# First loads and first products of a fused two-layer transformer kernel: keys' inputs loaded in four pieces each, products interleaved, bias row later, half the warm-up matmuls

## The reference, cut to what matters

```python
x = x + tanh(g_xattn[0]) * L0_xattn(layernorm(x), ctx, ctx)        # causal attention, 16 heads of 32
x = x + tanh(g_ffn[0])   * L0_ffn(layernorm(x), w_gate_up, w_proj) # weights rounded to -1, 0, 1 by groups of 64
x = x + tanh(g_xattn[1]) * L1_xattn(layernorm(x), ctx, ...)        # projections q, k_img, v_img, o
x = x + tanh(g_ffn[1])   * L1_ffn(layernorm(x), w_norm, w_gv, w_out)
```

## Time and profile before

| | us |
|---|---|
| median of 3 runs | 1070.06 (1070.04 to 1070.12) |
| profiled execution, whole time | 1070.2 |
| its span, first to last instruction | 1068.4 |
| PE busy | 1037.9 (97%) |
| DVE busy | 832.5 (78%) |
| ACT busy | 585.7 (55%) |
| POOL busy | 119.4 (11%) |

### The profile page before, as it was taken

How to read it: one execution, slowest core, us unless ns; L and a number is a source line. 1 busy time by engine, 2 the same in 40 slices (tenths; PEclk the granted TensorE clock), 3 DMA queues, 4 the chain that set the end, 5 groups by cost and what they waited for, 6 DMA issues and landing times.

```text
span 1068.4 us, 24253 instructions
## 1 busy us (share of the span) xinstructions
PE 1037.9 (97%) x9685; PEld 616.8 (58%) x9770; DVE 832.5 (78%) x1440; ACT 585.7 (55%) x893; POOL 119.4 (11%) x212
## 2 busy tenths in 40 slices
PE   8899999999999999999999999999999999999998
PEld 3555555555777777777777664444444444444444
DVE  4988888878777675675666487798898989888987
ACT  4766777677443332333333357647585858583633
POOL 1101001010000000000000211221111111110110
DMA  9575554542331130321311032224343434331223
GB/s 363 172 256 173 195 182 138 187 146 74 121 80 45 46 80 1 80 65 36 80 32 49 20 93 57 62 47 91 80 90 80 90 79 89 78 69 44 41 59 80
DMA packets 121200, 102.77 MB, mean 96 GB/s; under 512 B 94721, under 2 KB 95233, under 8 KB 120833
## 3 DMA queue, kind: packets, MB, share of 16 engines
q1 hardware_dynamic: 121088, 101.21, 34.4%
HBM read 65.54 MB, written 12.58 MB: 73 GB/s over the span
## 4 chain that ended last, share of the span: by engine, by line
PE 82%; DVE 9%; issue 4%; ACT 2%; DMA 2%; SPq 0%; POOL 0%; ACTq 0%; DVEq 0%; POOLq 0%
PE bank L704 10%; PE bank L705 10%; PE bank L792 10%; PE bank L669 9%; PE bank L810 9%; PE bank L918 7%; PE bank L936 4%; PE bank L906 4%; PE bank L869 3%; PE bank L891 2%; PE bank L549 2%; PE bank L606 2%; PE bank L574 2%; PE bank L622 2%; PE bank L634 2%
## 5 line engine op out<-in xcount | busy, mean ns | idle before, releaser
L704 PE MATMUL bank<-ARENA,W 128*128 128x256 f16 x1024 | 227.3, 273 | 0.7 <-issue 0.7
L705 PE MATMUL bank<-ARENA,W 128*128 128x256 f16 x1024 | 227.3, 273 | 0.0
L1111 ACT ACTIVATE ARENA<-ARENA 128x512 f16<-128x512 f32 (+1 forms) x96 | 66.8, 707 | 140.1 <-DVE ARENA L1759 132.0
L918 PE MATMUL bank<-W,ARENA 128*128 128x512 bf16 x496 | 115.8, 379 | 3.1 <-DMA ARENA<-ARENA 0.6
L810 PE MATMUL bank<-ARENA 128*128 128x512 f32 x256 | 118.4, 603 | 0.2 <-DVE ARENA L1846 0.2
L669 PE MATMUL bank<-ARENA 128*128 128x512 f32 x256 | 117.8, 602 | 0.7 <-DMA ARENA<-in_wkv 0.7
L792 PE MATMUL bank<-W,ARENA 128*128 128x512 bf16 x478 | 114.1, 379 | 2.6 <-DVE ARENA L1765 0.6
L704 PEld LDWEIGHTS bank<-ARENA,W 128*128 128x128 bf16 x1024 | 100.2, 98 | 19.2 <-issue 1.1
L705 PEld LDWEIGHTS bank<-ARENA,W 128*128 128x128 bf16 x1024 | 100.2, 98 | 17.9
L2224 POOL TENSOR_TENSOR ARENA<-ARENA 128x2 f32<-128x2 f32 (+1 forms) x72 | 51.7, 718 | 481.0 <-DVE ARENA L1533 249.1
L1759 DVE SCALAR_TENSOR_TENSOR ARENA<-bank,ARENA 128x512 f32<-128x512 f32 x64 | 48.0, 749 | 65.7 <-PE bank L705 62.3
(11 more groups left out here) (190 smaller groups left out, 1730.8 us busy)
## 6 DMA issues: line engine op xcount, KB each, us to landing
W<-in_w SPq DMA_DIRECT2D x48, 512.0 KB, 4.2
ARENA<-in_w SPq DMA_DIRECT2D x24, 512.0 KB, 3.6
kv_store<-ARENA SPq DMA_DIRECT2D x32, 256.0 KB, 4.4
W<-kv_store SPq DMA_DIRECT2D x15, 512.0 KB, 4.5
ARENA<-in_ctxT SPq DMA_DIRECT2D x8, 512.0 KB, 3.8
X<-in_x SPq DMA_DIRECT2D x8, 512.0 KB, 6.7
ARENA<-in_ctx SPq DMA_DIRECT2D x8, 512.0 KB, 6.2
out<-X SPq DMA_DIRECT2D x15, 256.0 KB, 2.3
```

Of the source, the lines that this page charges most:

```text
L704: pe.matmul(bank[:, i * S:(i + 1) * S], W0[:, at:at + P], xt_half(b, 0)[:, k, :], start=(k == 0), stop=False)
L705: mm = pe.matmul(bank[:, i * S:(i + 1) * S], W0[:, at:at + P], xt_half(b, 1)[:, k, :], start=False, stop=(k == KD - 1))
L918: mm = pe.matmul(to, QQ[d][:, t, k * P:(k + 1) * P], W1[:, at:at + D], start=(k == 0), stop=(k == KD - 1))
L1111: return act.activation(to, src, ACT.Copy)
```

## The change

`load_keys(0)` and the two halves of the key weights become eight smaller loads: for each `k` of 0 to 3, the 256 columns of the turned context and the 512 columns of the weights that step `k` needs. The bias row goes from between them to behind the columns. The products of the two token tiles are interleaved: step 0 of both, step 1 of both, and so on, and each step waits for its own two pieces. The warm-up has five matmuls in place of ten. There are three new semaphores; nothing else is computed or moved.

```diff
-            load_keys(0)
-            sp.dma_start(bufA["wkv"][:, 0, 0:2 * D], wkv[:, 0:2 * D]).then_inc(s.ld_wk, 16)
-            sp.dma_start(keep["row"], vec[:, 0:D]).then_inc(s.ld_kb, 16)
-            sp.dma_start(bufA["wkv"][:, 0, 2 * D:KD * D], wkv[:, 2 * D:KD * D]).then_inc(s.ld_wk2, 16)
+            for k, (keys, weights) in enumerate(((s.ld_p0, s.ld_p0), (s.ld_p1, s.ld_wk), (s.ld_p2, s.ld_p2), (s.ld_kt0, s.ld_wk2))):
+                sp.dma_start(bufA["KT"][:, k, :], ctxT[:, k * S:(k + 1) * S]).then_inc(keys, 16)
+                sp.dma_start(bufA["wkv"][:, 0, k * D:(k + 1) * D], wkv[:, k * D:(k + 1) * D]).then_inc(weights, 16)
             load_x(0)
             sp.dma_start(pre["cst"], cst).then_inc(s.ld_cst, 16)
             sp.dma_start(keep["gate"], gates).then_inc(s.ld_gc, 16)
             sp.dma_start(keep["cols"], cols).then_inc(s.ld_gc, 16)
+            sp.dma_start(keep["row"], vec[:, 0:D]).then_inc(s.ld_kb, 16)
             load_w0(0)
...
-                pe.wait_ge((s.ld_wk, s.ld_wv)[what], 16)
-                pe.wait_ge((s.ld_kt0, s.ld_kt1)[b % 2], 16 * (b // 2 + 1))
+                if (b, what) != (0, 0):
+                    pe.wait_ge((s.ld_wk, s.ld_wv)[what], 16)
+                    pe.wait_ge((s.ld_kt0, s.ld_kt1)[b % 2], 16 * (b // 2 + 1))
...
                 for k in ks:
-                    if not what and k == 2:
-                        pe.wait_ge(s.ld_wk2, 16)
+                    if (b, what) == (0, 0):
+                        for landed, pieces in (((s.ld_p0, 2),), ((s.ld_p1, 1), (s.ld_wk, 1)), ((s.ld_p2, 2),), ((s.ld_kt0, 1), (s.ld_wk2, 1)))[k]:
+                            pe.wait_ge(landed, 16 * pieces)
...
-            for n in range(10):
+            for n in range(5):
                 pe.matmul(banks[7], bufA["MHL"][:, 0, :], bufA["MHL"].rearrange("p a b -> p (a b)"), start=True, stop=True)
-            a_project(0, 0, 0)
-            a_project(0, 0, 1)
+            for k in range(KD):
+                a_project(0, 0, 0, (k,))
+                a_project(0, 0, 1, (k,))
```

More of the change, by code:

```diff
@@ L39 @@
 Sems = namedtuple("Sems", """
-    ld_cst ld_gc ld_x0 ld_x1 ld_kt0 ld_kt1 ld_rv0 ld_rv1 ld_w00 ld_w01 ld_w02 ld_w1a ld_w1b ld_wk ld_wk2 ld_wv ld_sel ld_wqo ld_kb ld_row ld_wn
+    ld_cst ld_gc ld_x0 ld_x1 ld_kt0 ld_kt1 ld_rv0 ld_rv1 ld_w00 ld_w01 ld_w02 ld_w1a ld_w1b ld_wk ld_wk2 ld_p0 ld_p1 ld_p2 ld_wv ld_sel ld_wqo ld_kb ld_row ld_wn
 ld_k0 ld_k1 ld_v0 ld_v1 st_kv0 st_kv1 st_out0 st_out1
```

## The result

The changed kernel takes 1072.33 us (median of 14 runs, 1071.47 to 1075.47) against 1070.09 of the kernel before (14 runs, 1069.59 to 1073.06). The ratio is 1.0023, interval 1.0016 to 1.0031. The forecast was 1070.4 and its range ended at 1071.5, so it was wrong. The runs fall into groups: six lie at 1071.5 to 1071.6, five between 1072.0 and 1073.9, and three at 1075.3 to 1075.5. The profiled execution is one of the last group (1075.47, span 1073.7). The mean clock granted to TensorE sorts them too: the four runs in which it is 1.000 all lie at 1071.47 to 1071.62, the ten with 0.997 or 0.998 reach from 1071.61 to 1075.47.

The account below looks back on a forecast made before the run. PE's own work, busy 97% of the span, was taken as the bound, with only the start movable. Scores gained 0.1, but the later store's +0.3 replaced it: 1070.06 + 0.3 = 1070.4 us, range 1069.0 to 1071.5.

Parts of the forecast that it names:

- The later issue is covered by the backlog: SP's eight issues ahead of x: full DMA traffic hides x's later issue; otherwise x up to 1.9 us later.
- bound of 1.2 us late for x: Landing of x: forecast 0.2 us earlier, at worst 1.2 later if the late issue shows, 1.9 - 0.7.
- after 10 us: Start of x's statistics: later than 10 us would say that the issues bound the traffic; 9.4 to 9.8 expected.
- It costs and brings nothing by itself: Warm-up: five matmuls less, 2.2 us of PE work, only fill time in which PE waits for loads.
- Side by side: Interleaved key products: tile 0 ends 0.9 us before tile 1, at 10.5; no change visible behind ACT's copy.
- Size of packets: Smaller packets of key weights and context: +0.43 and +0.14, together +0.57 us for everything behind; +0.5 taken.
- Bias row: Bias row's load behind the columns lands at some 11 us; POOL needs it only after 12.5, so no cost.
- Store backlog: Store releasing ACT's copy at 33.01 lands 0.5 us later; DVE's maxima come 0.3 us later, the last wait.
- Second rival: PE's pause from 11.4 to 14.0 drops the clock to 1.2 GHz; scores 2.1 us later, 1072.2; chance 0.09.
- First: Rival: traffic goes by bytes, x comes 0.7 us earlier without a later store; 1069.9; chance 0.26.
- third: Rival: PE's own work bounds the front, so all 2.4 us gained go to the end; 1067.7; chance 0.05.
- fourth rival: Pieces share traffic evenly, so the first pair lands with the others at 5.6; time 1070.4 as forecast; chance 0.10.

Follow-up runs that it names:

- both `wqo` variants: Changed kernel with the 2 MB load of query and output weights issued behind the last stores, 1071.78 us, or cut into eight of 256 KB, 1072.07 us.
- one by one: Changed kernel with its two first key products one after the other instead of interleaved; 1071.96 us.
- ten warm-ups with fillers: Changed kernel with ten warm-up matmuls and twelve matmuls of zeros between the first products and the turn of x; 1071.63 us.
- the old loads: Changed kernel with the context whole and key weights in two halves, three loads in place of eight; 1073.16 us.
- the two queues: Changed kernel with the four key weight pieces issued from ACT's queue beside SP's four context pieces; 1073.13 us.
- the better version with `wqo` later: Kernel before with bias row later, third store ahead of two 512 KB loads, and the query and output weights' load issued later; 1069.46 us.
- the early store with and without the rest of the change: Third key/value store issued ahead of two 512 KB loads: in the changed kernel 1072.21 us; in the kernel before, with bias row later, 1069.33 us.

## Why the prediction was wrong, step by step

- **"The later issue is covered by the backlog": this failed first.** A backlog never formed: an issue of 0.47 us brought a piece of 128 or 256 KB, 192 KB on average and 0.42 MB per us, about the 406 GB/s that the DMA engines move, so the loads were carried off as fast as they were issued. The traffic fell to 222 GB/s at 5 to 6 us, the first 10 us moved 0.39 MB less, and the back of the queue is 1 us late. For x the parts are now measured, the split between packets and issues in one profile: the row -1.3 (8.53), the packets at most +0.7 (9.20), the issues at least +1.1 (10.29); the working had -0.7, +0.5 and 0. Its bound of 1.2 us late for x would have held them. Further back the same error weighs more, because the row's gain is not there to set against it. For everything behind the pieces the working had +0.5 (packets) and 0 (issues); the selector's cast and the third unit of `w0` came 1.09 late. The statistics of x at 10.29 are the sign that the prediction named for this ("after 10 us").
- **"It costs and brings nothing by itself", on the warm-up: failed.** Five matmuls less in the kernel before cost 1.5 us of the median, by the ratio 0.2 to 2.1, and 0.7 us at the scores. In the changed kernel the products, taken at 0.45 us a record from their start, ran at the lower clock until about 8.3. The prediction had read the 4.45 us of the warm-up as all at the lower clock and the products as all at the upper, but did not ask what the products would run at when only 2.3 us of work lay ahead of them.
- **Side by side: the order was right, the cost not seen.** ACT's first copy started at 12.65, not 10.5; in the kernel before the order costs 0.2 us or more at the scores, covered by the store.
- **Size of packets: the term of 0.57 is not refuted.** At most 0.7 us is left for it. Whether pieces of 1 and 2 KB a row cost anything, where the Trainium skill (DMA: Bandwidth & Descriptors, Specifications) gives 512 bytes as enough for line rate, these runs leave open: 369 against 378 GB/s in 4 to 9 us is nearly the full rate, and the 0.7 us hold an unknown part of issue time.
- **Bias row: no cost, as said, and its gain eaten by the store where it stands alone.**
- **Store backlog: the right place, the wrong size.** The working named the copy at 33.01 as the last wait and moved it by 0.5 to 33.5. It measured 34.35, +1.34. Nor is it the backlog alone that times it: SP issues the store only when ACT has the signs of the third unit of `w0`, and this wait carried the delay of the loads over to the store's issue, +1.10. This and the clock behind it are what the trace shows at the last wait of the front.
- **Second rival (the clock): right mechanism, at another place.** In the changed kernel PE pauses only 0.41 us ahead of the turn, because its products, cold up to about 8.3, end only at 13.4. Where the products are warm, as with ten warm-ups, the pause of 2.41 us came and cost 1.37 us at the scores, against 2.1 worked out. In the changed kernel the clock fell at 35 us instead, in a pause that the late store made. No rival had that.
- **First, third and fourth rival:** traffic by bytes and a bound by PE are excluded by x at 10.29 and scores at 19.82. The first pair landed ahead of the rest, at 4.39.
- **The stop at 272** was not foreseen and could not be read from the profile of before, which has no stop; it is in the one run of the slowest group that has a profile.

Added up for the median: the small loads alone +1.5 (0.4 to 2.4 by the ratio), five warm-ups alone +1.5 (0.2 to 2.1); the whole is +2.2 (1.7 to 3.3). So the two parts overlap: both delay the same scores, and in both profiles the store lands about 1 us later, with five warm-ups for no reason that a run shows. The lowest group of the runs is +1.5 (1071.6 against 1070.1); that clock and stop make the rest is argued from the mean clocks and from one profile.

What stays open is when the clock falls. In profiles with a pause of 1.7 to 2.6 us ahead of the third scores, the clock fell in four (the changed kernel, both `wqo` variants, bias row alone) and stayed up in two (one by one 1.79, ten warm-ups with fillers 2.30). Ahead of the next scores a pause of 1.91 us stands in five profiles, and it fell behind three (the old loads, the two queues, the better version with `wqo` later) and stayed up behind two (the early store with and without the rest of the change). What tells them apart was not found.

## What to carry to other kernels

Before cutting a load into pieces, divide the size of a piece by the time of an issue: with 0.47 us an issue, loads of 128 to 256 KB left the DMA engines partly idle (share 0.66), and in a start whose traffic is full for 30 us the idle stretch was paid at the far end of the queue. A warm-up that seems to fill idle time has to be judged by the clock of the work behind it, and a pause gained in front of a later wait can bring the clock down. An early gain was worth nothing until the next fixed landing, here a store, had been moved as well: the row alone gave 1.3 us at the scores and nothing at the end, and with the store 1 us, of which the interval leaves 0.2 to 2.0.

## What the runs showed of the hardware

- The page's PEclk reads 1.00 while warm-up matmuls take 0.44 us in place of 0.24, so a clock of 1.00 near the start is not evidence. Later it does show 0.50, as here in the changed kernel at 36 to 37 us:

```profile
36.00:37.00 1.00, 1.00 (x16) 0.35 (x16) 0.00 (x0) 1.00 (x3) 0.36 (x1) 0.50 0.06 16
```

- PE stood still for 2.38 us without any semaphore in two profiles, the two of seventeen in which a 16 KB packet of the instruction queue, seen at 264 to 270 us in the others, comes at 272 to 276.
- A DVE multiplication of 128x1024 bf16 takes 0.69 us alone and 1.65 beside POOL's addition of 128x512 f32.
- The same store of 256 KB, issued between 22.6 and 24.8 us, takes 9.5 to 10.8 us to land in traffic that is full up to 32 us.
